# Self-attention of a decoder layer: projections in halves, the shift transposed before it is negated and split, maxima four steps ahead

## What is computed

```python
qkv = x @ qkv_w + qkv_b
q, k, v = jnp.moveaxis(qkv.reshape(b, n, 3, H, D), 2, 0)
attn = jnp.einsum('bnhd,bmhd->bhnm', q, k) * scale
attn = jax.nn.softmax(attn, axis=-1)
out = jnp.einsum('bhnm,bmhd->bnhd', attn, v).reshape(b, n, c)
```

## Time and profile before

| | us |
|---|---|
| median of 3 runs | 3607.77 |
| lowest and highest run | 3606.08, 3609.77 |
| profiled execution, its own time | 3603.72 |
| its span | 3601.9 |
| granted clock, mean share of 2.4 GHz | 0.974 |

### The profile page before, as it was taken

How to read it: one execution, slowest core, us unless ns; L and a number is a source line. 1 busy time by engine, 2 the same in 40 slices (tenths; PEclk the granted TensorE clock), 3 DMA queues, 4 the chain that set the end, 5 groups by cost and what they waited for, 6 DMA issues and landing times. The chain is left out here.

```text
span 3601.9 us, 50083 instructions
## 1 busy us (share of the span) xinstructions
PE 3402.7 (94%) x18021; PEld 2203.4 (61%) x18021; DVE 2511.9 (70%) x4512; ACT 1673.9 (46%) x3043; POOL 1996.7 (55%) x1008
## 2 busy tenths in 40 slices
PE   7999999999999999999999997999959999999995
PEld 5545455455455555555454435688838889988885
DVE  5777777777777777777777754689844676556676
ACT  2555555555555555555555564344422333233342
POOL 2688989888888888898889870011120011101112
PEclk9999999999999999999999998999969999999997
DMA  6322222321322312312211021223232243233342
GB/s 224 106 56 66 72 67 73 91 60 60 94 68 62 98 51 69 103 40 87 84 51 42 13 84 54 74 83 98 71 112 78 92 144 115 82 105 130 136 136 93
DMA packets 190268, 308.34 MB, mean 86 GB/s; under 512 B 25513, under 2 KB 72233, under 8 KB 190010
## 3 DMA queue, kind: packets, MB, share of 16 engines
q1 hardware_dynamic: 166970, 243.82, 22.1%
q0 software_dynamic: 14592, 44.32, 3.5%
q10 hardware_dynamic: 8448, 16.78, 1.3%
HBM read 195.66 MB, written 61.33 MB: 71 GB/s over the span
## 5 line engine op out<-in xcount | busy, mean ns | idle before, releaser
L511 DVE TENSOR_REDUCE sa_part_max<-sa_mx 128x1 f32<-128x512 f32 x2048 | 1281.1, 679 | 540.8 <-PE sa_mx L625 536.9
L466 ACT ACTIVATE sa_prob<-sa_sc 128x512 f32<-128x512 f32 x2010 | 1101.5, 595 | 803.3 <-PE sa_sc L692 763.4
L268 POOL TENSOR_TENSOR sa_quad_sum<-sa_quad_sum,sa_prob 128x1024 f32<-128x1024 f32 x500 | 1174.8, 2381 | 5.4 <-ACT sa_prob L466 5.4
L268 POOL TENSOR_TENSOR sa_quad_sum<-sa_prob 128x1024 f32<-128x1024 f32 x250 | 588.4, 2373 | 267.4 <-ACT sa_prob L466 267.4
L625 PE MATMUL sa_mx<-sa_k_even,sa_q_stack 96*128 96x512 f32 x1024 | 490.2, 482 | 16.8 <-DVE sa_part_max L511 7.5
L625 PE MATMUL sa_mx<-sa_k_odd,sa_q_stack 96*128 96x512 f32 x1024 | 477.1, 466 | 9.9 <-DVE sa_part_max L511 8.5
L692 PE MATMUL sa_sc<-sa_q_stack,sa_k_even 98*128 98x512 f32 x1024 | 428.3, 418 | 0.0
L2093 PE MATMUL ex_acc<-ex_w,ex_hT 128*128 128x512 f32 x1719 | 415.2, 392 | 2.5 <-DVE ex_hT L2004 2.3
L692 PE MATMUL sa_sc<-sa_q_stack,sa_k_odd 98*128 98x512 f32 x986 | 415.5, 423 | 1.6 <-ACT sa_prob L466 1.6
L2093 PEld LDWEIGHTS ex_acc<-ex_w,ex_hT 128*128 128x128 f32 x1719 | 318.8, 188 | 66.5 <-issue 4.9
L625 PEld LDWEIGHTS sa_mx<-sa_k_even,sa_q_stack 96*128 96x128 f32 x1024 | 195.5, 191 | 193.0 <-issue 102.6
(11 more groups left out here) (231 smaller groups left out, 4050.8 us busy)
## 6 DMA issues: line engine op xcount, KB each, us to landing
ex_w_in<-in_L_ffn_w_dram SPq DMA_DIRECT2D x130, 512.0 KB, 4.3
sa_xT<-xT SPq DMA_DIRECT2D x57, 1024.0 KB, 5.2
sa_q_stack<-sa_hilo SPq DMA_DIRECT2D x372, 64.0 KB, 2.0
rows<-sa_empty SPq DMA_DIRECT2D x48, 257.0 KB, 3.9
ex_rows<-rows POOLq DMA_DIRECT2D x8, 1542.0 KB, 7.7
sa_k_odd<-sa_hilo SPq DMA_DIRECT2D x192, 64.0 KB, 2.0
ex_xg<-rows POOLq DMA_DIRECT2D x48, 256.0 KB, 3.1
sa_k_even<-sa_hilo SPq DMA_DIRECT2D x168, 64.0 KB, 2.0
```

The source lines that it names most:

```text
L268: pool.tensor_tensor(quad_sum[:, i % 2, heads, :], so_far, prob[:, k, heads, :], ALU.add).then_inc(quad_ready, 1)
L466: act.activation(prob[:, kt % 4, j, :], score_bank(n)[:, :], ACT.Exp, scale=SCALE).then_inc(prob_ready, 1)
L511: dve.reduce_max(part_max[:, q, j, k:k + 1], mx[n % 3][:, :], AX_X).then_inc(max_read, 1)
```

## The change

Four things are changed together.

- The projection parts become eight halves each (`project_half`): for q and k one slice of input channels for 256 of the 512 columns, for v two of the four matmuls of a row tile. HALVES_AT puts 24 halves a chunk behind single heads of the steps 0 to 15, none of them right ahead of a burst. The operations leave PSUM at step 4, at step 10 and at step 0 of the next chunk. The order of OPS is changed to fit: v of the third tile moves to the last place of the unit.
- `top` is transposed as it is (4 rows for each quarter instead of 8), into the next of the three `mx` banks, which it takes for one turn (SHIFT_PLACE, `place_of_max`, `max_bank_free`), behind the second head of step 12. DVE then negates and splits it on the way out of PSUM, in two operations in place of one copy. L520 and L522 and the tile `shift` are gone.
- EARLY is 4 instead of 3, so the maxima run one step further ahead, `part_max` has two buffers, and 16 instead of 12 maxima stand ahead of the first chunk.
- The inversions come in two pairs behind the second head of steps 6 and 8, the division one group of four steps later, the store at step 13.

```diff
-    EARLY = 3
+    EARLY = 4
...
-    SUMS_AT, DENS_AT, DIVIDE_AT, STORE_AT = 0, 2, (1, 1), 10
-    INVERT_AT = ((3, 1), (3, 3), (4, 1), (4, 3))
+    SUMS_AT, DENS_AT, DIVIDE_AT, STORE_AT = 0, 2, (2, 1), 13
+    INVERT_AT = {(6, 1): (0, 1), (8, 1): (2, 3)}
+    SHIFT_AT = (12, 1)
...
-           Op("q", 3, 0, 1, 3), Op("k", 2, 1, 1, 4), Op("v", 2, 1, 1, 4),
-           Op("k", 3, 1, 2, 5), Op("q", 0, 1, 2, 6), Op("v", 3, 1, 2, 5),
-           Op("v", 0, 1, 3, 6), Op("q", 1, 1, 3, 7), Op("v", 1, 1, 3, 7)]
-    PARTS_AT = ((0, 1, 2, 3), (4, 5, 6, 7), (8, 9, 10, 11))
+           Op("q", 3, 0, 1, 3), Op("k", 2, 1, 1, 4), Op("k", 3, 1, 1, 5),
+           Op("q", 0, 1, 2, 6), Op("v", 3, 1, 2, 5), Op("v", 0, 1, 2, 6),
+           Op("q", 1, 1, 3, 7), Op("v", 1, 1, 3, 7), Op("v", 2, 1, 3, 8)]
+
+    HALVES_AT = (((0, 3), (1, 1), (1, 2), (1, 3), (2, 2), (2, 3), (3, 1), (3, 3)),
+                 ((4, 3), (5, 1), (5, 3), (6, 3), (7, 1), (7, 3), (8, 3), (9, 1)),
+                 ((10, 3), (11, 1), (11, 3), (12, 3), (13, 1), (13, 3), (14, 3), (15, 1)))
+    LEAVE_STEPS = (4, 10, T)
 
...
+    MAXIMA_TO_SHIFT = LEAD + SHIFT_AT[0] * PER_STEP + SHIFT_AT[1] + 1
+    SHIFT_PLACE = {min(g * NMAX + MAXIMA_TO_SHIFT, CHUNKS * NMAX) + g - 1: g for g in range(1, CHUNKS)}
+    PLACE_OF_SHIFT = {g: place for place, g in SHIFT_PLACE.items()}
...
+    def place_of_max(n):
+
+        return n + max((n - MAXIMA_TO_SHIFT) // NMAX, 0)
...
-    part_max = r.sb("part_max", [P, TQ, HG, KQ])
+    part_max = r.sb("part_max", [P, 2, TQ, HG, KQ])
     top = r.sb("top", [P, TQ, HG])
-    shift = r.sb("shift", [P, TQ, HG, 2], F32R)
-    shiftT = r.sb("shiftT", [2 * HG, BANK], F32R)
+    shiftT = r.sb("shiftT", [HG, 2, BANK], F32R)
...
+    def max_bank_free(engine, place):
+
+        old = place - len(mx)
+        if old in SHIFT_PLACE:
+            engine.wait_ge(shiftT_ready, SHIFT_PLACE[old] + 1)
+        elif old >= 0:
+            engine.wait_ge(max_read, old + 1 - sum(1 for other in SHIFT_PLACE if other < old))
...
-                             shiftT[2 * j:2 * j + 2, :].bitcast(F32)).then_inc(shift_in, 16)
+                             shiftT[j:j + 1, :, :].bitcast(F32)).then_inc(shift_in, 16)
...
-            dve.reduce_max(part_max[:, q, j, k:k + 1], mx[n % 3][:, :], AX_X).then_inc(max_read, 1)
+            dve.reduce_max(part_max[:, n // NMAX % 2, q, j, k:k + 1], mx[place_of_max(n) % len(mx)][:, :], AX_X).then_inc(max_read, 1)
...
-            dve.reduce_max(top[:, :, :], part_max[:, :, :, :], AX_X).then_inc(top_ready, 1)
-
             after(dve, shift_mm, g)
-            dve.wait_ge(top_ready, g + 1)
-            dve.tensor_scalar(shift[:, :, :, 0], top[:, :, :], -1.0, None, ALU.mult).then_inc(shift_hi, 1)
-            dve.wait_ge(shift_hi, g + 1)
-            dve.scalar_tensor_tensor(out=shift[:, :, :, 1], in0=top[:, :, :], scalar=-1.0,
-                                     in1=shift[:, :, :, 0].bitcast(F32), op0=ALU.mult, op1=ALU.subtract).then_inc(shift_ready, 1)
+            dve.reduce_max(top[:, :, :], part_max[:, g % 2, :, :, :], AX_X).then_inc(top_ready, 1)
 
         def leave_shift(g):
             dve.wait_ge(shift_mm, g + 1)
 
             after(dve, shift_in, g * 16 * HG)
-            dve.tensor_copy(shiftT[:, :], misc[0:2 * HG, :]).then_inc(shiftT_ready, 1)
+            bank = mx[PLACE_OF_SHIFT[g] % len(mx)] if g > 0 else misc
+            dve.tensor_scalar(shiftT[:, 0, :], bank[0:HG, :], -1.0, None, ALU.mult).then_inc(shift_hi, 1)
+            dve.wait_ge(shift_hi, g + 1)
+            dve.scalar_tensor_tensor(out=shiftT[:, 1, :], in0=bank[0:HG, :], scalar=-1.0, in1=shiftT[:, 0, :].bitcast(F32),
+                                     op0=ALU.mult, op1=ALU.subtract).then_inc(shiftT_ready, 1)
 
...
-                    if i == 0 and kt == T - EARLY + 1 and g + 1 < CHUNKS:
+                    if (kt, i) == SHIFT_AT:
                         leave_shift(g + 1)
                     if i == 1 and (g, kt) in LEAVE_AT:
                         leave_psum(LEAVE_AT[g, kt])
-                    if (kt, i) in INVERT_AT and g > 0:
-                        invert(g - 1, INVERT_AT.index((kt, i)))
+                    if g > 0:
+                        for q in INVERT_AT.get((kt, i), ()):
+                            invert(g - 1, q)
                 if kt == T - EARLY - 1 and g + 1 < CHUNKS:
...
+        def project_half(i, half):
+
+            job = JOBS[i]
+            slot = job.load % 2
+            if half == 0:
+                if job.what == "q":
+                    pe.wait_ge(in_wq, (job.unit + 1) * 16 * KC)
+                else:
+                    pe.wait_ge(in_wkv, (job.unit + 1) * 16 * (KC + 1))
+                after(pe, in_x[slot], 16 * loads_until(job.load))
+
+                if JOBS[i - 1].place is None:
+                    pe.wait_ge(shiftT_ready, 1)
+                else:
+                    pe.wait_ge(v_ready if JOBS[i - 1].what == "v" else hilo_ready, left_psum(i - 1))
+            if job.what == "v":
+                t = half // 2
+                for k in (0, 1) if half % 2 == 0 else (2, 3):
+                    last = pe.matmul(misc[:, t * P:(t + 1) * P], xT[:, slot, k, t * P:(t + 1) * P], wkv[:, k, 1, :],
+                                     start=(k == 0), stop=(k == KC - 1))
+            else:
+                k = half % KC
+                cols = slice(half // KC * (BANK // 2), (half // KC + 1) * (BANK // 2))
+                weight = wq[:, k, :] if job.what == "q" else wkv[:, k, 0, :]
+                last = pe.matmul(misc[:, cols], weight, xT[:, slot, k, cols], start=(k == 0), stop=(k == KC - 1))
+            if half == 2 * KC - 1:
+                last.then_inc(proj_mm, 1)
+
         def max_pass(n, m, g):
 
-            after(pe, max_read, n - 2)
+            place = place_of_max(n)
+            max_bank_free(pe, place)
             q, j, k = m // (HG * KQ), m // KQ % HG, m % KQ
             at = g % NQ * BANK + q * P
-            pe.matmul(mx[n % 3][:, :], q_stack[0:QK, j, at:at + P], k_stack[g // NQ % 2][0:QK, j, k * BANK:(k + 1) * BANK],
+            pe.matmul(mx[place % len(mx)][:, :], q_stack[0:QK, j, at:at + P], k_stack[g // NQ % 2][0:QK, j, k * BANK:(k + 1) * BANK],
                       start=True, stop=True).then_inc(max_mm, 1)
 
         def transpose_shift(g):
 
-            pe.wait_ge(shift_ready, g + 1)
+            if g > 0:
+                max_bank_free(pe, PLACE_OF_SHIFT[g])
+            bank = mx[PLACE_OF_SHIFT[g] % len(mx)] if g > 0 else misc
+            pe.wait_ge(top_ready, g + 1)
             for q in range(TQ):
-                last = pe.transpose(misc[0:2 * HG, q * P:(q + 1) * P],
-                                    shift[:, q, :, :].bitcast(F32).rearrange("p j a -> p (j a)"), ident[:, :])
+                last = pe.transpose(bank[0:HG, q * P:(q + 1) * P], top[:, q, :], ident[:, :])
             last.then_inc(shift_mm, 1)
 
...
                         max_pass(n, n % NMAX, n // NMAX)
                     score(g, kt, i)
+                    if (kt, i) == SHIFT_AT and g + 1 < CHUNKS:
+                        transpose_shift(g + 1)
                     if g < LAST or kt <= 2:
                         if i == 1 and kt % 2 == 0:
                             burst(g, kt)
                     elif i == HG - 1:
                         last_burst(kt)
-                    if i == 2 and kt == T - EARLY and g + 1 < CHUNKS:
-                        transpose_shift(g + 1)
-                if (g, kt) in PART_AT:
-                    project_part(*PART_AT[g, kt])
+                    if (g, kt, i) in HALF_AT:
+                        project_half(*HALF_AT[g, kt, i])
         for g in range(LAST):
```

More of the change, by code:

```diff
@@ L125, in self_attention @@
     JOBS = [Job(0, what, n, None, None, None) for what, n in FIRST_OPS]
-    JOBS += [Job(u + o.ahead, o.what, o.n, u * NQ + o.c, u * len(LOADS) + o.load, PARTS_AT[i % 3])
+    JOBS += [Job(u + o.ahead, o.what, o.n, u * NQ + o.c, u * len(LOADS) + o.load, i % 3)
              for u in range(UNITS) for i, o in enumerate(OPS) if u + o.ahead < UNITS]
@@ L129, in self_attention @@
     VALUES = [i for i, job in enumerate(JOBS) if job.what == "v"]
-    PART_AT = {(job.chunk, kt): (i, part) for i, job in enumerate(JOBS) if job.place for part, kt in enumerate(job.place)}
-    LEAVE_AT = {(job.chunk, job.place[-1] + 1): i for i, job in enumerate(JOBS) if job.place}
+    HALF_AT = {(job.chunk, kt, j): (i, half) for i, job in enumerate(JOBS) if job.place is not None
+               for half, (kt, j) in enumerate(HALVES_AT[job.place])}
+    LEAVE_AT = {divmod(job.chunk * T + LEAVE_STEPS[job.place], T): i for i, job in enumerate(JOBS) if job.place is not None}
+    MAXIMA_TO_SHIFT = LEAD + SHIFT_AT[0] * PER_STEP + SHIFT_AT[1] + 1
+    SHIFT_PLACE = {min(g * NMAX + MAXIMA_TO_SHIFT, CHUNKS * NMAX) + g - 1: g for g in range(1, CHUNKS)}
+    PLACE_OF_SHIFT = {g: place for place, g in SHIFT_PLACE.items()}
     USERS = {}
@@ L203, in self_attention @@
```

(21 more changed lines are left out.)

1 line of the change is left out of this document (removed).

## The result

The changed kernel takes 3480.6 us (median of 4 runs, 3478.7 to 3482.6), the kernel before 3606.9 us beside it: a ratio of 0.965 (95% interval 0.9635 to 0.9658), 126 us less. The forecast was 3488 us.

A forecast was written before the change was run, and what follows sets the result against it. PE bounds self-attention: 60.6 us of work in a 65.03 us chunk, the other 4.4 waits. Terms -108 (chunks 0 to 27), -12 (28 to 30) and +0.5 (start) give -119.5, so 3488 us; range 3468 to 3530, 8 in 10.

The forecast's parts named there:

- The sum of 60.6 us a chunk: PE's work in a chunk of the kernel before: pairs 29.9, bursts 16.5, row sums 3.4, parts 10.4, transposes 0.45.
- The two added terms: Chunks 0 to 27: 0.1 us a chunk for starting v halves, 0.5 for two runs of four pairs left without a half.
- rival B: Doubled weight loads of q and k show in PE's time: 1.8 us a chunk, +49, 3537 us; chance 0.07.
- The 0.26 us of a run of four pairs: With two score banks, the third score matmul waits 0.26 for the first exponential; left at (10,0) and (0,0).
- Rival A: Pacing stays in part: half the eight windows keep 0.26, PE waits 0.4 for `top`; 62.6 a chunk, 3527 us; chance 0.15.
- the 93%: A sign that the forecast holds: POOL busy over 93% of a chunk.
- The 108 us: Gain over chunks 0 to 27: 61.2 us a chunk against 65.03, 3.85 less, times 28.
- The waits of DVE at steps 4 and 5: PE waits 0.35 and 0.7 us where the first projection's leaving and the reciprocals meet on DVE; this 1.05 would go.
- the 0.4 "that I could not place": Of PE's 4.4 us of waits a chunk, 0.4 in pieces, such as shift transposes behind DVE and chunk start.
- 59 us a chunk and one fall of the clock: Chunks 28 to 30: 64.0 falls to about 59 without L520 and L522, one clock fall costs 2 to 3; 12 us won.
- The term was +0.5: Before chunk 0: four more maxima, 2.4 us, fit into PE's 2.90 wait for shift rows, which come 0.5 later.
- Rival C: Chunk starts wait for shift rows behind the store in SP's queue: +42 above before, 3650 us; chance 0.05.

The follow-up runs named there:

- one_transpose: The changed kernel with `top` kept as head x quarter and transposed in one piece of 16 rows instead of four of 4: 3475.3 us, ratio 0.963.
- split_first: The changed kernel with the old order of the shift: DVE negates and splits `top` from SBUF to SBUF before PE transposes it: 3732.7 us, ratio 1.034.
- quarters: The kernel with one transposition of 16 rows, plus quarters of projection halves behind (9,3) and (15,3): 3466.7 us, ratio 0.961.

## Why the prediction was right, and where not

**Built from record ends, PE's work held.** The sum of 60.6 us a chunk, with 0.1 and 0.5 added, gave 61.2; the period is 61.30. The two added terms are confirmed: the halves cost 0.06 us a chunk more than parts (I had 0.1 for v and nothing for the loads), so rival B is out. The Trainium skill (TensorE: Matmul & The Clock Gate, "Part 3: Packing small matmuls — row/col tiling") says that a weight load overlaps a running matmul only when its row group differs; that doesn't agree with 0.06 us for 16 more loads of these matmuls. The 0.26 us of a run of four pairs stands where it was placed, disappears where a quarter is put in, and comes back in the number foretold when the halves are doubled up. Rival A needed it in places where it isn't. POOL is busy 94% of the time between 464.7 and 1752.1 us, over the 93% that the prediction names as a sign.

**28 chunks times the period was a little too generous.** The 108 us took 65.03 for chunk 0 as well; it took 63.3, and it won 2.6. The 27 others won 3.7 each instead of 3.85. So this term was 6 us too large and that of chunks 28 to 30, below, 11 too small: that the total came so close owes something to luck.

**The waits of DVE at steps 4 and 5 had about the right size, but the shares don't add up.** The sum had 1.05 us for the earlier trace rows. Moved in the kernel before, the reciprocals win 1.0 on average in these two steps and, with the shift rows out of the store's way, 0.91 of the period (65.03 to 64.12). Put back in the changed kernel they cost 1.76. With the 2.6 of the doubled halves that makes 4.4, more than the 3.7 won: the two losses overlap, and no share of the 3.7 can be given to each. Where the 0.4 "that I could not place" lies is open. The maxima bank for the transposes, the new steps of leaving, the order of OPS and the later division and store were not tried one by one.

**Chunks 28 to 30: right mechanism, half the size.** I gave 59 us a chunk and one fall of the clock, 180 us for the three. They take 58.3, 58.3 and 56.0, 172.7, and the clock doesn't fall; it falls once at the start of chunk 31, for 3.2 us. That is 7 of the 11 us missing. The other 4 lie in what the sum starts from: I had 64.0 us a chunk before, from the shift's copy, where the first exponentials give 195.9 for the three. POOL, busy 98%, is close to being the bound, as said, but that is read from its share alone. In one_transpose and quarters, where POOL's work is the same, chunks 28 and 29 fall to 58.0, so it isn't POOL alone. Of the 23 us won here no run takes away L520 alone. That it is the cause of most of it rests on PE's waits for it, 9.1 us in all and each with a low clock around it, on split_first, where the same operation, put back, costs 8.1 us in every chunk, and on the 64 us a chunk that stay in the kernel before when only its reciprocals and its store are moved.

**The start.** The term was +0.5, and the table shows +1.5. But 1.35 of it is there long before the maxima of which the term speaks, in PE's wait for the first rows of q:

```profile
43.64 0.73 PE L665 MATMUL sa_mx<-sa_k_even,sa_q_stack 96*128 96x512 f32 x2 [2.53 <-DMA sa_q_stack<-sa_hilo]
```

In the kernel before this wait ends at 42.29, and in the other runs anywhere from 41.96 to 43.70. From its end to the first exponential it is 67.4 us before and 67.6 after, so the change itself costs 0.1. The first maxima matmul of chunk 0 waits 0.29 us for the rows instead of 2.90: the additional maxima went into that wait, as I had reckoned, and the rows are sent 0.2 us later from the same point (60.83 instead of 60.63), not 0.5.

**Rival C did not happen in this kernel** but is real: see the run with the moved reciprocals. The shift rows of one chunk are sent from 1141.71 to 1144.2, and the next chunk starts at 1152.7: 8.5 us later, about 6.5 in hand if they land in 2 us as the moves of the earlier trace rows do. With one step less lead it still holds.

**The order of negation and transposition** was costed in the prediction as a gain in chunks 28 to 30 only. That was the largest thing that it missed: it is worth 8 us in every chunk as soon as the shift is taken at step 12. The forecast came out right since the change has the new order; for the old order with the rest of the change it would have been off by 250 us.

## What to carry to other kernels

Sum an engine's work from the distances between record ends, not from busy time, and compare it with the period: the difference is what rearranging can win, and a bank pair's wait shows as one longer record at a fixed place. Cut filler work finely enough to stand wherever a run of dependent pairs would outlast its banks, and put the other engines' extra work where the bound engine is in a long burst. Before a small transfer or a small SBUF-to-SBUF operation is moved, look at what it lands behind: 1.5 us in SP's queue gave back all that the moved reciprocals had won, and a 0.18 us operation took 6 us under a run of POOL's additions.
